# A gated cross-attention and spiking feed-forward block: the first batch's first products reordered, and the last channels made in units of 256, 128 and 128 tokens

## The reference

```
q = ln(x) @ Wq;  k, v = split(concat([ln(ctx), ln(x)]) @ Wkv)       # 974 keys
x = x + tanh(g_xattn) * (softmax(8 * q k^T) v) @ Wout
h = relu(ln(x) @ W_fc.T) ** 2                                       # width 2048
y = h @ W_proj.T
for 5 steps:  mem = 0.9 * mem + y - (mem > 1);  spikes += (mem > 1)
out = x + tanh(g_ffn) * spikes / 5
```

## Time and profile before

| what | us |
|---|---|
| median of 3 runs | 1052.84 |
| lowest and highest | 1051.77 and 1054.56 |
| the profiled execution, its own time | 1051.86 |
| its span, first to last instruction | 1050.1 |
| PE (matmul) busy | 1031.7 (98%) |
| PEld (weight loads) busy | 843.4 (80%) |
| DVE busy | 792.4 (75%) |
| ACT busy | 593.6 (57%) |
| POOL (GpSimd) busy | 314.1 (30%) |

### The profile page before, as it was taken

The page is one execution under the profiler, slowest core; times in us unless marked ns, Lnnn a source line. Parts: engine busy times, 40 slices in busy tenths (PEclk is TensorE's granted clock), DMA queues, the critical chain, the costliest instruction groups (busy, mean ns, idle before and its releaser), DMA issues.

```text
span 1050.1 us, 19058 instructions
## 1 busy us (share of the span) xinstructions
PE 1031.7 (98%) x6945; PEld 843.4 (80%) x6945; DVE 792.4 (75%) x1227; ACT 593.6 (57%) x1147; POOL 314.1 (30%) x289
## 2 busy tenths in 40 slices
PE   6999999999999999999999999999999999999997
PEld 5878778878877877887887787777788888998886
DVE  7488879987987987998798798779434555584766
ACT  6558447656654844765665484466446433445535
POOL 4333633345434363334543436334000000000000
PEclk9999999999999999999999999999999999999999
DMA  6302010100201201010020200122430001201011
GB/s 196 135 1 78 2 36 27 49 9 26 76 0 35 76 0 35 28 48 9 26 76 0 75 0 0 35 91 61 148 120 21 1 1 40 82 1 41 22 61 41
DMA packets 31891, 47.43 MB, mean 45 GB/s; under 512 B 2284, under 2 KB 11516, under 8 KB 31852
## 3 DMA queue, kind: packets, MB, share of 16 engines
q1 hardware_dynamic: 31716, 46.74, 13.7%
q10 hardware_dynamic: 136, 0.17, 0.1%
HBM read 39.56 MB, written 7.34 MB: 45 GB/s over the span
## 4 chain that ended last, share of the span: by engine, by line
PE 96%; DVE 2%; DMA 1%; issue 0%; ACT 0%; ACTq 0%; DVEq 0%
PE work L490 42%; PE work L643 14%; PE score L656 13%; PE heads_out L595 9%; PE score L569 9%; PE score L505 2%; PE heads_out L607 1%; PE score L842 1%; DMA vectors<-in_L_xattn_bl 1%; PE maxes L582 1%; PE heads_out L490 1%; PE score L776 1%; DVE on L1419 0%; PE maxes L577 0%; PE maxes L784 0%
## 5 line engine op out<-in xcount | busy, mean ns | idle before, releaser
L1836 POOL TENSOR_TENSOR dsum<-dsum,probs 125x448 f32<-125x448 f32 x186 | 221.2, 1189 | 14.6
L490 PE MATMUL work<-wv,xT 128*125 128x512 f32 (+1 forms) x768 | 187.0, 397 | 0.0
L490 PE MATMUL work<-xT,wk 128*128 128x486 f32 (+2 forms) x768 | 184.1, 390 | 0.5 <-DVE kst L1384 0.5
L490 PEld LDWEIGHTS work<-wv,xT 128*125 128x125 f32 (+1 forms) x768 | 137.9, 183 | 37.4 <-issue 2.3
L490 PEld LDWEIGHTS work<-xT,wk 128*128 128x128 f32 x768 | 140.3, 188 | 30.1 <-issue 4.6
L643 PE MATMUL work<-zT,wf 128*128 128x512 f32 (+1 forms) x768 | 164.1, 364 | 0.0
L643 PEld LDWEIGHTS work<-zT,wf 128*128 128x128 f32 x768 | 131.5, 189 | 23.0 <-issue 0.7
L962 ACT ACTIVATE probs<-score 125x448 f32<-125x448 f32 (+1 forms) x256 | 119.8, 548 | 46.2 <-PE score L569 46.1
L1833 POOL TENSOR_TENSOR dsum<-probs 125x448 f32<-125x448 f32 x31 | 41.0, 1322 | 340.2 <-ACT probs L968 340.2
L1372 DVE TENSOR_TENSOR probs<-probs,maxes 125x1792 f32<-125x1792 f32 x64 | 128.4, 2017 | 1.1
L656 PE MATMUL score<-hT,wp 128*128 128x512 f32 (+1 forms) x576 | 117.4, 354 | 0.0
(11 more groups left out here) (196 smaller groups left out, 1440.3 us busy)
## 6 DMA issues: line engine op xcount, KB each, us to landing
xin<-in_ctx SPq DMA_DIRECT2D x42, 250.0 KB
neuron<-in_L_ffn_W_fc SPq DMA_DIRECT2D x16, 256.0 KB, 2.9
neuron<-in_L_ffn_W_proj SPq DMA_DIRECT2D x16, 256.0 KB, 2.9
xres<-in_x SPq DMA_DIRECT2D x16, 224.0 KB, 2.6
x_scratch<-xres SPq DMA_DIRECT2D x16, 224.0 KB, 2.5
xin<-in_x SPq DMA_DIRECT2D x14, 224.0 KB, 10.0
zt<-x_scratch SPq DMA_DIRECT2D x3, 1024.0 KB, 5.6
fin<-x_scratch SPq DMA_DIRECT2D x3, 1024.0 KB, 5.6
```

The lines of the kernel that those rows point to most:

```text
L490: mm = pe.matmul(bank, lhs(i, k), rhs(j, k), start=(n == 0), stop=(n == len(passes) * chunks - 1))
L1836: pool.tensor_tensor(total[0:ROWS[t]], total[0:ROWS[t]], tile(t), ALU.add).then_inc(dchain if t < TILES - 1 else dsum_done, 1)
```

## The change

At the start, TensorE makes the first half of the keys of channel block 0 right after the transposes of tiles 0 to 3, chunk by chunk as the high parts of `xT` come (`first_keys`), with three warming transposes of the identity between the chunks, and only then transposes tiles 4 to 7. The 32 warming transposes become 6 ahead of the first tile and 21 within `first_keys`. Its twelve products are the same as before, in the same three passes. ACT splits Wk chunks 0 and 1 before it takes the gains, and chunks 2 and 3 before it normalises tile 2; it takes the first keys out of their bank before it takes tiles 4 to 7, with Wq's chunks 2 and 3 split one before and one after these tiles. DVE splits its Wk chunks after the statistics of the second pair, and takes the first keys between its first two chunks of Wq, ahead of tiles 4 to 7.

At the end, the last block of channels has three units: 256, 128 and 128 rows. The two small ones have banks 0 and 1, and 48 matmuls of 128 columns each. The sums of unit 2 are put in after hidden block 6 of unit 4's products and those of unit 3 after block 12 of unit 5's. Units 4 and 5 are summed by `last_back`, which waits for each step's spikes by itself and not for all five at the start. The last block's store becomes three DMAs, of 256, 128 and 128 rows.

```diff
-    UNITS = [(0, 0, TG, 0), (1, 0, TG, 1), (2, 0, TG, 2), (3, 0, TG // 2, 3), (3, TG // 2, TG // 2, 0)]
+    UNITS = [(0, 0, TG, 0), (1, 0, TG, 1), (2, 0, TG, 2), (3, 0, TG // 2, 3), (3, TG // 2, P, 0), (3, TG // 2 + P, P, 1)]
...
-                for i in range(2):
-                    two = slice(2 * i, 2 * i + 2)
+                for i, part in enumerate((slice(0, 2), slice(2, 3), slice(3, 4))):
                     sp.wait_ge(fin_done, T0[FINAL] + DC + i)
-                    sp.dma_start(rows[:, two, cut:D], fin[:, two, cut:D]).then_inc(fin_out, 16)
+                    sp.dma_start(rows[:, part, cut:D], fin[:, part, cut:D]).then_inc(fin_out, 16)
...
+            def first_keys():
+
+                bank = work[0][:, 0:XO + HALF]
+                pe.wait_ge(ends_hi, 2)
+                for k in range(DC):
+                    pe.wait_ge(w_hi, k + 1)
+                    pe.wait_ge(xhi_done, k + 1)
+                    pe.matmul(bank, wk[:, 0, k, 0:P], xT[:, 0, k, 0:XO + HALF], start=(k == 0), stop=False)
+                    warm(3)
+                pe.wait_ge(w_lo[0], DC)
+                for k in range(DC):
+                    pe.matmul(bank, wk[:, 1, k, 0:P], xT[:, 0, k, 0:XO + HALF], start=False, stop=False)
+                for k in range(DC):
+                    pe.wait_ge(xlo_done, k + 1)
+                    mm = pe.matmul(bank, wk[:, 0, k, 0:P], xT[:, 1, k, 0:XO + HALF], start=False, stop=(k == DC - 1))
+                    if k < DC - 1:
+                        warm(3)
+                mm.then_inc(kq_mm, 1)
...
+            warm(6)
             first_transposes(0, 1, 2, 3)
-            warm(32)
-            pe.wait_ge(w_lo[0], DC)
+            first_keys()
             first_transposes(4, 5, 6, 7)
-            keys_queries(0, 0, (0,), first=True)
             keys_queries(0, 1, (0,), first=True)
...
-                if bank == 0:
-                    pe.wait_ge(y_done, FINAL * DC + 1)
+                if bank < 2:
+                    pe.wait_ge(y_done, FINAL * DC + (bank + 1))
...
+            def last_back(u):
+
+                d, at, n, _ = UNITS[u]
+                bank = (maxes, heads_out)[(T0[FINAL] + u) % 2]
+                pe.wait_ge(fin_done, T0[FINAL] + u - 1)
+                for k in range(5):
+                    if k < 4:
+                        pe.wait_ge(step_spk, 4 * (u - 1) + k + 1)
+                    else:
+                        pe.wait_ge(spk_done, FINAL * 2 + (u + 1))
+                    mm = pe.matmul(bank[:, 0:P], step_spikes(u)[:, k, :] if k < 4 else
+                                   spikes[:, d * TG + at:d * TG + at + n], ident_b[:, :], start=(k == 0), stop=(k == 4))
+                mm.then_inc(spkT_mm, 1)
...
-                last_down(TG // 2, TG // 2, 0, back=2, after=11)
-                unit_back(3)
-                unit_back(4)
+                last_down(TG // 2, P, 0, back=2, after=6)
+                last_down(TG // 2 + P, P, 1, back=3, after=12)
+                last_back(4)
+                last_back(5)
...
+            split_hi(0, wk, 0, 1)
             act.wait_ge(vec_mm, 1)
...
             first_norm(0)
-            split_hi(0, wk, 0, 1)
+            split_hi(0, wk, 2, 3)
             first_norm(2)
-            split_hi(0, wk, 2, 3)
             hi_chunks(0, 0, 0, 1, 2, 3)
             first_norm(5)
             first_norm(7)
             split_hi(1, wq, 0, 1)
+            kq_hi_parts(0, 0, 0, first=True)
+            split_hi(1, wq, 2)
             hi_chunks(0, 1, 0, 1, 2, 3)
-            kq_hi_parts(0, 0, 0, first=True)
-            split_hi(1, wq, 2, 3)
+            split_hi(1, wq, 3)
             kq_hi_parts(0, 1, 0, first=True)
...
             first_statistics(1)
+            split_lo(0, wk, 0, 1)
             dve.wait_ge(gain_ready, 1)
...
-            split_lo(0, wk, 0, 1)
             first_statistics(2)
             first_statistics(3)
             lo_chunks(0, 0)
-            split_lo(1, wq, 0, 1)
+            split_lo(1, wq, 0)
+            kq_lo_parts(0, 0, 0, first=True)
+            split_lo(1, wq, 1)
             lo_chunks(0, 1)
-            kq_lo_parts(0, 0, 0, first=True)
...
                 finish_unit(3)
+                unit_steps(5, 0, 9)
                 finish_unit(4)
+                finish_unit(5)
```

More of the change, by code:

```diff
@@ L479, in _ @@
             store_units()
-            sp.wait_ge(fin_out, T0[GROUPS] * 16)
+            sp.wait_ge(fin_out, (T0[GROUPS] + 1) * 16)
         @block.tensor
```

## The result

The median of 20 runs is 1054.8 us (1054.05 to 1056.23), that of 20 runs of the kernel before is 1052.82. The ratio is 1.0020, with a 95% interval of 1.0015 to 1.0026: **slower, by 2.0 us**, but by less than the 0.3% named as the bound. The forecast was 1055.5 with a range of 1052.3 to 1057.6. The profiled execution took 1054.2 with a span of 1052.4, 2.3 over the span before.

What follows compares the result with a forecast made beforehand. The prediction took PE to bound the kernel (96% of the chain). Head -0.4 and tail +3.05 gave +2.65 us, on the earlier median of 1052.84 a forecast of 1055.5 us, range 1052.3 to 1057.6.

Steps and rivals of the forecast that it cites:

- What bounds it: Whole kernel: time is when PE becomes continuously busy, plus PE's own work, plus what follows the last product; chain 96% PE.
- Head, the start: Head up to tiles 4 to 7: tile 0 at 10.6, first high part at 13.5 (13.1 to 13.7), their transposes at 19.3.
- The stall that takes its place: Head, before the first keys' second half: PE idles about 1.1 us until DVE's low parts at 24.8; PE gains 0.4 us.
- Tail, the pitch: Last channels: 96 products of 128 columns at 0.110 each, set by the weight load, make PE 5.45 us later.
- The steps behind it: After PE's last product: shorter copy, DVE steps at 0.33, one product left and a shorter sum save 2.3 us.
- The store: End of the tail: a last store of 64 KB in place of 128 saves perhaps 0.1 us.
- The sum: Whole kernel: head -0.4 and tail +3.05 make +2.65 us.
- a pitch from columns: Rival, tail: columns set the pitch at 0.07, so tail -1.1, total -1.5, time 1051.3; chance 0.09.
- one of 0.08: Rival, tail: a pitch of about 0.08, a load taking less behind longer products; total -0.25, time 1052.6; chance 0.10.
- load and product in series: Rival, tail: weight load and product run one after the other, +7.9 - 0.4, time 1060.3; chance 0.04.
- The clock rival: Rival, head: TensorE falls to 1.2 GHz, so the head loses some 2 us, time 1057.9; chance 0.08.

Runs made afterwards that it cites:

- run 6: Changed kernel without the nine warming transposes of the first keys' pass 3, then without all 21: 1054.34 and 1053.98 beside 1051.89, ratio 1.0018 for both.
- Run 7: Changed head with the old tail, transposes of tiles 4 to 7 taken chunk by chunk in place of nine warming ones: 1050.66 beside 1051.89, ratio 0.9986.
- run 3: Kernel before plus 96 extra products in eight shapes after the warming transposes: twelve with 128 weight columns took 1.5 us at 16, 64 and 128 data columns.
- the fastest kernel: Kernel before with chunk-by-chunk head and last unit of 256 summed step by step: 1050.00 beside 1051.89 (ratio 0.9980), then 1049.97 beside 1052.90 (0.9969).

## Why the prediction was right

**What bounds it**: shown. The chain is 96% PE before and after, PE's work from 33 to 1026 us is the same, and what the tail costs arrives in the time: the tail alone is 3.05 to its last sum in the trace and +2.9 by the ratio. The head's 0.4 is too small for any of the times to show.

**Head, the start.** Tile 0 was transposed from 10.57 (10.6 forecast). The clock rose within tile 2's transposes, so the high parts began at 13.25, between the bounds of 13.1 and 13.7, 0.25 under the value taken. That the clock rose so early was luck: of nine executions that have six early transposes this is the earliest rise, and in the changed kernel's second execution, at 1.2 GHz throughout the transposes, the high parts began at 14.03, beyond the later bound (0.3 of it by a later load). Pass 3 ended as PE's own work and not DVE's: the transposes followed at 19.18 (19.3), and taking work from PE there moved them (run 6).

**The stall that takes its place**: shown. It was 1.05 (1.1), it ended at 24.68 (24.8) on DVE's last low part, and the gain of 0.41 at the 0.46 hole is the 0.4 of the sum. Run 7 shows the mechanism: starting that chain earlier leaves 0.20 of the stall.

**Tail, the pitch**: 0.112 where 0.110 was taken, for the reason given, the load (run 3). PE's last product came 1016.90 after the hole's end where it came 1011.50 before, 5.40 later (5.45). The 5.45 has a slip in it: the steps as the prediction lists them, from 1034.37, add up to 1046.66 and not to 1046.76, so to 5.35. **The steps behind it**: copy and hand-over 0.51 (0.50), a DVE step 0.325 (0.33), last spikes to PE 0.29 (0.28), PE to the sum 0.35 (0.43), the sum 0.35. The 0.35 is with the clock still up, where a last product takes 0.23; in three of the five executions with this tail it takes 0.29, and PE to the sum is 0.40. **The store**: 2.0 from the last sum to the end of the span in place of 2.3; 0.1 had been taken for it. This 0.3 is the term that was sized too small. It comes back with this tail (2.0 in all five executions, and 2.2 to 2.3 in the seven whose last store has 128 KB), but the size of the last store alone doesn't give it: with units of 384 and 128 it is 64 KB too and the end is 2.5 behind the last sum. There SP issues its last two stores back to back, from 1048.28 and in 0.90, so the last goes out some 0.2 behind its sum (an estimate, half of the 0.90 each). So the tail is +3.0 to its last sum, where the steps add up to 3.15, and +2.7 to the end of the span.

**The sum** gave +2.65. The two profiled spans differ by 2.3, and the 0.35 between is 0.15 ahead of the last sum and 0.2 in the store. That the medians differ by 2.0 and not 2.3 is within the interval and was not pursued. The range of its own that the prediction gives to its forecast, 1053.9 to 1057.0, is not what its terms make: the head's -1.1 to +0.5 and the tail's 2.9 to 4.0 on 1052.84 are 1054.6 to 1057.3. The measured 1054.8 lies in both. The rivals: a pitch from columns and one of 0.08 are refuted by run 3, load and product in series by the 0.112. The clock rival did not come about: in the changed kernel a product costs 0.23 right before the hole, (2.90 - 0.38)/11, and behind it, and PEclk is 1.00 across it.

## What to carry to other kernels

Before cutting the last matmuls smaller so as to have a shorter chain behind them, price the small ones by what sets their pitch: where each has a fresh set of 128 fp32r weight columns, 128 data columns cost 0.112 and 256 cost 0.120, so the cut nearly doubles PE's time for the same products. Take the saving that is free of it first: here the step-by-step sum gave 0.9 us without any extra product. And where work is pulled forward into a wait, look at what the next consumer waits for: the first keys came 2.7 us of products early, but delayed the transposes of the other tiles, and only moving those forward too turned 0.4 us into 1.2 to 1.5.

## What the runs showed of the hardware that was not expected

**The clock fell while PE was never idle.** In run 3 PE issued a product every 0.11 us until the clock fell, the first 24 with only 16 and 64 data columns, the next twelve with 128. Its windows (PE and PEld busy, then PEclk, DMA share, GB/s):

```profile
18.10:20.80 2.70, 2.69 (x25) 2.70 (x25) 1.00 0.60 234
20.90:21.90 1.00, 1.00 (x11) 1.00 (x11) 1.00 0.08 16
22.00:24.40 2.40, 2.40 (x15) 2.40 (x14) 0.58 0.00 0
24.50:29.00 4.50, 4.50 (x47) 4.50 (x47) 0.86 0.00 0
```

The clock was at 2.4 GHz up to 21.9 and at 1.2 GHz for most of 22.0 to 24.4, where the products of 192 columns ran; it was back within those of 256. So a busy PE in a trace is no sign that the clock holds. Why it fell was not tested. In the changed kernel it did hold, in the stretch with the hole and in the nine us of 128-column products at 0.112 alike (windows with all engines, PEclk the third number from the end):

```profile
17.00:24.00 7.00, 6.63 (x44) 5.55 (x42) 5.64 (x13) 6.29 (x16) 1.31 (x2) 1.00 0.19 74
1037.00:1046.20 9.20, 9.20 (x94) 9.20 (x91) 5.23 (x15) 4.11 (x13) 0.00 (x0) 1.00 0.24 87
```

**The weight load seems to slow with the clock.** In the stretch at 1.2 GHz the products of 192 data columns started 0.213 apart, and so did the first of those of 256, though these have a third more columns; a transpose of 128 columns in the kernel before cost 0.21 at that level too. What these have in common is 128 weight columns, and 0.213 is about twice the 0.112 of 2.4 GHz. So at this level too the load, at half its speed, is what fits; the probe had no group of fewer weight columns there to show it.

**PEclk can read 1.00 where the clock is low.** The transposes of the kernel before cost 0.21 each from 10.4 to 13.9, yet its window there (PE and PEld of L776, then PEclk) reads 1.00:

```profile
12.00:13.00 1.00, 1.00 (x6) 0.86 (x5) 1.00 1.05 291
```

The same holds in every trace here up to the first rise. In the head the level is to be read from what a transpose or a product costs, as is done above.

**When the clock rises decides a part of the head.** The second execution of the changed kernel, timeline of PE:

```profile
10.86 3.67 PE L775 MATMUL score<-ident,xin 125*128 125x125 f32 x16 [0.60 <-ACT xin L1240]
14.86 0.74 PE L792 MATMUL work<-xT,wk 128*128 128x490 f32 x1 [0.32 <-ACT xT L1068]
...
20.19 1.79 PE L775 MATMUL score<-ident,xin 125*128 125x125 f32 x16
...
25.69 0.49 PE L489 MATMUL work<-xT,wk 128*128 128x486 f32 x1 [1.04 <-DVE xT L1501]
```

Here the 16 transposes of tiles 0 to 3 took 3.67 in place of 2.88, all at 1.2 GHz, although the six warming ones had run from 8.7 as in the first. The first product came 0.8 later (14.86), of which 0.3 is tile 0's later start (10.86), and the second half's products 1.0 later, at 25.69: more than the changed head's whole gain. In the second execution of the fastest kernel the clock rose later still, within pass 1. By what transposes and products cost, it rose between 12.5 and 18.6 us in the nine executions with six early transposes, and between 14.3 and 15.6 in the five with the order of before. So six early transposes do not bring it forward reliably, and no run here settled on what it depends.
